# A two-layer transformer block on eight cores: moving the next group's norm statistics behind the first output tile

## The reference

```python
x = x + _layernorm(_L0_attn_ref(_layernorm(x), W_qkv, W_out))     # 8 batches x 2048, H = 1024
x = x + _layernorm(_L0_ffn_ref(_layernorm(x), router_w, w1, b1, w2, b2))
# the FFN, per token (F = 4096, 8 router outputs, top 2):
router_probs = softmax(xt @ router_w)
top_k_probs, idx = top_k(router_probs, 2); top_k_probs /= sum(top_k_probs)
expert_out = gelu(xt @ w1 + b1) @ w2 + b2
out = expert_out * sum(combine)          # combine: the top-2 weights, one-hot
```

## Time and profile before

| | us |
|---|---|
| median of 3 runs (1851.04 to 1856.6) | 1853.78 |
| the profiled execution | 1852.67 |
| its span on the slowest core (core 3) | 1851.1 |
| spans of the eight cores | 1823.6 to 1851.1 |
| median of die 0, of die 1 | 1844.8, 1839.2 |
| PE busy in the span | 1442.8 (78%) |
| DVE busy, ACT busy | 593.9 (32%), 558.7 (30%) |

### The profile page before, as it was taken

The page is one execution under the profiler, slowest core; times in us unless marked ns, Lnnn a source line. Parts: engine busy times, 40 slices in busy tenths (PEclk is TensorE's granted clock), DMA queues, the critical chain, the costliest instruction groups (busy, mean ns, idle before and its releaser), DMA issues.

```text
span 1851.1 us, 19500 instructions; the slowest of 8 cores (1823.6 to 1851.1 us)
## 1 busy us (share of the span) xinstructions
PE 1442.8 (78%) x6816; PEld 647.2 (35%) x6816; DVE 593.9 (32%) x1102; ACT 558.7 (30%) x1181; POOL 57.8 (3%) x101
## 2 busy tenths in 40 slices
PE   0587878888788887878888888747778796797697
PEld 0233333333334333333333333323333342343343
DVE  0443444443333333333333333321231223213103
ACT  0402210320222333333333333334442353352433
POOL 1000000000000000000000000110000000000000
PEclk9989899999888889898888888878898898898898
DMA  9212101110400000111111111959212012001002
GB/s 146 54 29 46 46 18 29 23 23 0 86 7 1 29 29 29 29 29 29 29 29 29 29 29 30 159 120 174 48 49 65 0 46 69 1 24 46 23 1 80
DMA packets 51617, 81.55 MB, mean 44 GB/s; under 512 B 19648, under 2 KB 27840, under 8 KB 51520
## 3 DMA queue, kind: packets, MB, share of 16 engines
q0 software_dynamic: 27280, 50.35, 15.8%
q1 hardware_dynamic: 24240, 29.94, 5.0%
HBM read 97.08 MB, written 20.97 MB: 64 GB/s over the span
## 4 chain that ended last, share of the span: by engine, by line
PE 66%; DVE 13%; DMA 8%; issue 6%; ACT 5%; DVEq 0%; SPq 0%; POOL 0%; ACTq 0%; POOLq 0%
PE pAll L185 33%; PE pAll L160 31%; DMA qtile<-qs 3%; DMA xgb<-xo 3%; DVE ptb L750 2%; PE pAll L216 2%; DMA qs<-qstage 2%; DVE vt L496 2%; DVE xfg L439 1%; DVE m L677 1%; DVE sm L374 1%; DMA x2lt<-x2s 1%; PE pAll L1061 1%; DVE qstage L467 1%; DVE x2t L832 1%
## 5 line engine op out<-in xcount | busy, mean ns | idle before, releaser
L160 PE MATMUL pAll<-x2f,w1b 128*128 128x512 bf16 x1024 | 236.7, 394 | 55.0 <-ACT h1g L1170 50.2
L160 PE MATMUL pAll<-kf,qtile 128*128 128x512 bf16 x1024 | 258.8, 413 | 24.4 <-DMA qtile<-qs 19.1
L185 PE MATMUL pAll<-vt,ptb 128*128 128x512 bf16 x1024 | 226.3, 382 | 0.9 <-DVE ptb L750 0.9
L185 PE MATMUL pAll<-w2b,h1g 128*128 128x512 bf16 x1024 | 222.4, 379 | 4.1 <-ACT h1g L1170 4.1
L677 DVE TENSOR_REDUCE m<-pAll 128x1 f32<-128x512 f32 x128 | 88.5, 691 | 344.0 <-PE pAll L160 343.3
L160 PEld LDWEIGHTS pAll<-x2f,w1b 128*128 128x128 bf16 x1024 | 102.4, 101 | 187.2 <-issue 77.7
L160 PEld LDWEIGHTS pAll<-kf,qtile 128*128 128x128 bf16 x1024 | 106.1, 105 | 168.0 <-issue 71.8
L688 ACT ACTIVATE pbuf<-pAll,nb 128x512 bf16<-128x512 f32 x128 | 87.6, 685 | 251.6 <-DVE nb L682 251.6
L185 PEld LDWEIGHTS pAll<-w2b,h1g 128*128 128x128 bf16 x1024 | 100.1, 98 | 125.9 <-issue 6.7
L185 PEld LDWEIGHTS pAll<-vt,ptb 128*128 128x128 bf16 x1024 | 100.8, 99 | 123.7 <-issue 4.8
L185 PE MATMUL pAll<-wvb,xfg 128*128 128x512 bf16 x512 | 115.6, 379 | 35.4 <-DVE vt L496 35.4
(11 more groups left out here) (109 smaller groups left out, 1031.0 us busy)
## 6 DMA issues: line engine op xcount, KB each, us to landing
xrt<-xo POOLq DMA_DIRECT2D x16, 512.0 KB, 6.9
x2s<-x2t SPq DMA_DIRECT2D x16, 512.0 KB, 3.3
w1b<-w POOLq DMA_DIRECT2D x8, 1024.0 KB, 29.9
w2b<-w POOLq DMA_DIRECT2D x4, 2048.0 KB, 43.2
x2rt<-x2s SPq DMA_DIRECT2D x16, 512.0 KB, 4.2
y<-yt SPq DMA_DIRECT2D x16, 512.0 KB, 2.9
xgb<-xo POOLq DMA_DIRECT2D x16, 256.0 KB, 8.2
qs<-qstage POOLq DMA_DIRECT2D x16, 256.0 KB, 2.7
```

The costliest lines, as they stand in the source:

```text
L160: return e.matmul(o(), l(), r(), start=st, stop=sp)
L185: return e.matmul(o(), l(), r(), start=st, stop=sp)
```

## The change

The call of `c_stats(gc + 1)` moves from ahead of the four output tiles to behind the issue of tile 0's epilogue and store. Nothing is added or removed.

```diff
@@ -1176,8 +1176,6 @@
         cx2f_free[0] = E.ev("tS")
-        if gc + 1 < 4:
-            c_stats(gc + 1)
         for k in range(4):
             qt = gc * 4 + k
@@ -1232,6 +1230,8 @@
                                  waits=[ev_ya], inc="dSy")
+            if k == 0 and gc + 1 < 4:
+                c_stats(gc + 1)
             if k == 2 and gc + 1 < 4:
                 c_pass1(gc + 1)
```

## The result

The changed kernel took 1866.47 us (median of 10 runs) against 1852.73 us of the kernel before (10 runs on the same chip): ratio 1.0068, 95% interval 1.005 to 1.0087, or 9 to 16 us slower by the interval and 13.7 us by the medians. Forecast were 17.2 us, which lies just above that interval, and a time of 1871. Runs in a slower state of the chip, one of the changed kernel's ten (1987.68 us) among them, are left out of the ratio; without it the median is 1866.24 us.

What follows compares the result with a forecast made beforehand. Bound: PE waiting in pass 1 for casts behind tile 2's epilogue. Three delays of 5.7 us, 17.2 in all, took the profiled 1852.67 to 1869.9 us; 1.1 for the median gave 1871.0, range 1864 to 1878.

Steps and rivals of the forecast that it cites:

- The free place before, and nothing gained by leaving it: Before tile 0's copy: 12.9 us of ACT statistics beside tile 0's matmuls delay nothing, so removing them gains nothing.
- Tile 0's epilogue with the table load, 9.82 us to the end of the apply: On ACT after the gelus: tile 0's Ln now needs the 1.28 us table switch; apply ends 9.82 us after its copy.
- Row sums on the path, Ln at 17.1: On DVE behind tile 0's add: sums take 4.71 us from 11.3, so Ln starts 17.1 us after tile 0's copy.
- Tile 1's copy at 23.3, tile 2's at 33.35 instead of 27.63: On ACT, from tile 0's copy: tile 1's copy 9.5 us late behind the diagonals, tile 2's 5.7 us late.
- PE's wait from 9.97 to about 15.7: In pass 1, ahead of the third bank fill: PE's wait grows from 9.97 to about 15.7 us in three groups.
- 5.7 us per group, 17.2 in all: At the end of tile 2's epilogue: a 5.7 us delay reaches PE in three groups, 17.2 us in all.
- Nothing after it gives the time back: After pass 1: tile 3's epilogue and the next group's transfers recover none of the 5.7 us per group.
- slack swallows it: Rival, 4%: PE still sets tile 2's copy, at 16.7 us per tile of matmuls; median stays near 1854.
- Overlap: Rival, 5%: DVE's row sums cost nothing beside ACT's squares; loss 11.6 us, median 1865.
- The block costs more: Rival, 7%: second table load, drain or longer low clock; 7.0 us or more per group, median 1875 to 1878.
- The narrower 1867 to 1875: Whole kernel: the main forecast's own range of median time in us, held at 82%.
- lower bound: Statistics between tiles 0 and 1: with free row sums, Ln comes earlier; delay 3.9 us per group, 11.6 in all.

Runs made afterwards that it cites:

- Experiment 3: Changed kernel with an unused Ln ahead of tile 0's copy, taking the table load off the chain; ratio 1.025 (1.007 to 1.0431), resting on two runs.
- Experiments 1: Changed kernel with the four row sums and first two small DVE operations issued ahead of tile 0 again; ratio 1.0054, inconclusive (0.9891 to 1.0218).
- experiment 4: Changed kernel with every statistics row sum done twice on DVE for groups 1 to 3; 67.94 us from tile 0's to tile 3's first matmul, against 63.2.
- experiments 8 to 11: Kernel before, then changed, with unused matmuls in PE's pass 1 wait: first stretches 56.52, 62.25 us; then changed and before rerun unedited, ratio 1.0117.
- experiment 7: Changed kernel with the next group's pass 1 issued ahead of tile 2's epilogue; 52.98 us from tile 0's to tile 3's first matmul.

## Why the forecast was right, point by point

- **The free place before, and nothing gained by leaving it:** right. Tile 0's copy was released by PE in both kernels, and its idle time in front only grew, from 1.87 to 14.63 us.
- **Tile 0's epilogue with the table load, 9.82 us to the end of the apply:** right; measured 1361.72 + 1.24 - 1353.07 = 9.89. Experiment 3 takes the load away alone, and 1.28 us go.
- **Row sums on the path, Ln at 17.1:** measured 1370.11 - 1353.07 = 17.04. Experiments 1 and 4 change this term alone, by -1.75 and +4.5 us of PE's wait.
- **Tile 1's copy at 23.3, tile 2's at 33.35 instead of 27.63:** measured 23.04 and 33.18. The 0.26 us in the first is overlap at a boundary: consecutive ACT operations start before the one ahead has ended, and I had added 0.1 us there.
- **PE's wait from 9.97 to about 15.7:** measured 15.5 in groups 0 and 2, and 16.0 in group 1, where two short waits of 0.2 to 0.3 us more appear in the chain.
- **5.7 us per group, 17.2 in all:** a little too much; the first stretches give 5.4 and 16.2. The clock came back a little earlier inside pass 1 (before it was 0.50 nearly throughout), whose rest took 5.20 us in group 0 (1397.00 to 1402.20), against 5.47; I had allowed for up to half a microsecond in the other direction.
- **"Nothing after it gives the time back":** this step was off by 1.7 us of 17. The second stretches are 0.6 us shorter in three groups. The term is a clock effect by experiments 8 to 11, small, repeatable, and not worked out.
- **The rivals:** "slack swallows it" would have needed tile matmuls of 16.7 us; they took 13.99. The 0.84 of the attention tile in the earlier trace rows was a mean, of 5.4 us at 0.50 and 11.3 us at 1.00 (windows 1206.8:1212.2 and 1212.2:1223.5 on core 3), and no pace that a whole tile group could have kept. "Overlap" would have shown ACT not waiting for DVE; it waits 2.39 us. "The block costs more" needed a second load or a drain; there is one load, of 1.28 us. The longer wait added nothing to what the low clock costs behind it.
- **The range** of 1864 to 1878 held the 1866.47 us, in its lower part. The narrower 1867 to 1875 that I had given the forecast itself missed it by 0.5 us, and the "overlap" rival's 1865 is closer to it than my 1871. So the time alone does not choose between them; the stretches (5.4 us per group, against 3.9 of that rival) and experiments 1 and 4 do. The low side comes from the two points above, 2.7 us, and from the scatter of when cores reach phase C, for which the sum has no term.
- **A slip in the lower bound:** 3 x 3.9 is 11.7, not 11.6; nothing hangs on it.

## What to carry to other kernels

Work that lies in the slack of one wait can be moved only where the slack at the new place is at least as long; here 13 us of statistics moved from a place where PE was waited for anyway to a pipeline of epilogues with 3.8 us of slack per tile and two tiles to go, and the rest came out at PE. Count the chain from a fixed event through every engine in issue order, including sums that were done "for free" long ahead. Here 1.75 of their 4.6 us came back, since the rest lay beside ACT's squares; four more came back in full. And when a chain ends in an engine waiting for the first of a group of small operations, look at what they stand behind: here the real gain, 10.7 us per group, was to issue the casts ahead of the epilogue.

## What the runs showed of the hardware

- A wait of PE of 15.5 us costs no more in low clock than one of 9.97 us: the rest of pass 1 behind it took 5.2 us against 5.5, and 5.5 us behind a wait of 20.03 (experiment 4). Behind 5.41 us (experiment 7) it took 4.9. With the wait filled by unused matmuls, the granted clock was 1.00 throughout and it ran in 4.1 us.
- Filling that wait saves 1.2 us per group in the first stretch of the kernel before (56.52 against 57.76), and the second is no shorter for it (90.94 against 90.96). In the changed kernel 0.9 us are saved in the first (62.25 against 63.17) and 0.9 us lost in the second (91.26 against 90.40).
- Time taken out of one stretch can be lost in the next by the clock: with the table load gone, the first stretch was 1.0 us shorter and the second 0.9 us longer in the mean, with 17.1 us of it at half clock instead of 12.9, and the three groups took 460.6 us against 460.7.
